# Attention phase of a Flamingo block: order of statistics, normalisation, residual and x transposes within a step

## What is computed

```python
x = x + tanh(g_xattn) * attention(layernorm(x), ctx, ctx, w_q, w_k, w_v, w_o)
x = x + tanh(g_ffn)   * ffn(layernorm(x), w_gate, w_up, w_down)

def attention(query, key, value, ...):
    scores  = q @ k.T * SCALE + causal mask (k_pos <= q_pos)
    weights = softmax(scores)
    return (weights @ v) @ w_o

def ffn(x, ...):                       # act_qdq: to 16-bit steps of the tensor's maximum and back
    up   = act_qdq(act_qdq(x) @ dequant4(w_up).T)
    gate = act_qdq(act_qdq(x) @ dequant4(w_gate).T)
    o    = act_qdq(act_qdq(gate * sigmoid(gate)) * up)
    return o @ dequant4(w_down).T
```

## Time and profile before

| | |
|---|---|
| three runs | 1492.4, 1486.42, 1490.44 us; median 1490.44 |
| the profiled execution | 1487.6 us, its span 1485.8 us |
| busy over the span: TensorE, VectorE, ScalarE, GpSimd | 89%, 69%, 43%, 17% |
| mean granted TensorE clock | 0.956 of full |
| TensorE's waits for another engine, 0 to 560 us, the three largest | 13.3, 9.2 and 6.9 us |

### The profile page before, as it was taken

The page is one execution under the profiler, slowest core; times in us unless marked ns, Lnnn a source line. Parts: engine busy times, 40 slices in busy tenths (PEclk is TensorE's granted clock), DMA queues, the critical chain, the costliest instruction groups (busy, mean ns, idle before and its releaser), DMA issues. The chain is left out here.

```text
span 1485.8 us, 18879 instructions
## 1 busy us (share of the span) xinstructions
PE 1328.3 (89%) x6142; PEld 1086.8 (73%) x6142; DVE 1021.9 (69%) x1397; ACT 644.8 (43%) x769; POOL 255.1 (17%) x312
## 2 busy tenths in 40 slices
PE   7899999999999978999999999999992029999999
PEld 6677767768777866888888778878882018888887
DVE  0467667856866655777777679998998984545453
ACT  2434334334333324333333255556667973333331
POOL 1124214313312220001000034550110000000000
PEclk9999999999999998999999999999996559999999
DMA  8013202312322435666764889986558863454543
GB/s 311 1 36 100 93 30 92 99 42 71 106 70 69 171 123 209 246 238 237 247 240 159 271 295 311 319 311 214 174 202 334 316 223 116 161 167 150 176 145 118
DMA packets 111248, 259.77 MB, mean 175 GB/s; under 512 B 10832, under 2 KB 23120, under 8 KB 109648
## 3 DMA queue, kind: packets, MB, share of 16 engines
q1 hardware_dynamic: 110896, 259.04, 50.3%
q10 hardware_dynamic: 288, 0.00, 0.0%
HBM read 152.04 MB, written 106.95 MB: 174 GB/s over the span
## 5 line engine op out<-in xcount | busy, mean ns | idle before, releaser
L1096 PE MATMUL gpG<-xph,Wh 128*128 128x512 f32 x384 | 153.0, 398 | 6.0 <-DVE xpl L1020 6.0
L1570 PE MATMUL pD<-Wh,xph 128*128 128x512 f32 x384 | 150.7, 392 | 4.6 <-DVE xpl L1549 4.6
L1096 PE MATMUL pU<-xph,Wh 128*128 128x512 f32 x384 | 150.8, 393 | 1.7 <-POOLq L63 1.0
L1096 PE MATMUL gpG<-xph,Wl 128*128 128x512 f32 x384 | 150.8, 393 | 0.0
L1096 PE MATMUL gpG<-xpl,Wh 128*128 128x512 f32 x384 | 150.6, 392 | 0.0
L1570 PE MATMUL pD<-Wh,xpl 128*128 128x512 f32 x384 | 150.5, 392 | 0.0
L1570 PE MATMUL pD<-Wl,xph 128*128 128x512 f32 x384 | 150.5, 392 | 0.0
L1096 PE MATMUL pU<-xpl,Wh 128*128 128x512 f32 x384 | 150.2, 391 | 0.0
L1096 PE MATMUL pU<-xph,Wl 128*128 128x512 f32 x384 | 150.1, 391 | 0.0
L1549 DVE TENSOR_TENSOR xpl<-doq,xph 128x1536 fp32r<-128x1536 int16 (+1 forms) x34 | 56.4, 1663 | 123.1 <-ACT xph L1516 123.1
L1003 ACT ACTIVATE gst<-gpG,sc 128x512 f32<-128x512 f32 x96 | 66.3, 691 | 168.3 <-PE gpG L1096 168.3
(11 more groups left out here) (172 smaller groups left out, 2930.5 us busy)
## 6 DMA issues: line engine op xcount, KB each, us to landing
dub<-up_d SPq DMA_DIRECT2D x42, 768.0 KB, 4.7
gate_d<-gst SPq DMA_DIRECT2D x96, 256.0 KB, 2.3
gb<-gate_d SPq DMA_DIRECT2D x32, 768.0 KB, 6.3
up_d<-ust SPq DMA_DIRECT2D x96, 256.0 KB, 4.3
xr<-xn_d SPq DMA_DIRECT2D x9, 1024.0 KB, 6.0
xph<-up_d SPq DMA_DIRECT2D x11, 768.0 KB, 6.2
xpl<-up_d SPq DMA_DIRECT2D x11, 768.0 KB, 6.0
xin<-in_x SPq DMA_DIRECT2D x32, 256.0 KB, 2.7
```

Of the source, the lines that this page charges most:

```text
L1096: mm = pe.matmul(ps[:, :], Ws[:, it, kt * P:(kt + 1) * P], xs[:, kt, :], start=(kt == 0 and Ws is Wh and xs is xh), stop=(kt == KT - 1 and ...
L1570: mm = pe.matmul(pD[4 * t + q][:, :], os_[n][:, cs], Ws[:, it, :], start=(it == 0 and os_ is oh and Ws is Wh), stop=(it == IT - 1 and os_ ...
```

## The change

Six orders within a step are changed. GpSimd does `rstd` of tile k+2 ahead of that of tile k-3. ScalarE normalises tile k+2 directly after the probability copies and the job's copy, no longer at the end of the step. VectorE takes the statistics of tile k+2 at the head of the step, and in an A-chunk step the residual ahead of them; the sums come ahead of the job's scale; in a chunk step all corrections come ahead of `largest`. TensorE turns x ahead of the values in an A-chunk step too, with one wait more, ahead of the second chunk, for the second half of `pTl`.

```diff
--- before.py
+++ after.py
@@ -507,10 +507,10 @@
                 pool.tensor_scalar(rs_[:, n, 2:3], mv_[:, n, 0:1], rs_[:, n, 1:2], -1.0, ALU.mult, ALU.mult).then_inc(rstd_s, 1)
 
             def step(b, k, have, jobs):
+                if have(k + 2):
+                    rstd(b, k + 2, mv, rs, mean_done, eps_done, rstd_done, xn_done)
                 if have(k - 3):
                     rstd(b, k - 3, mv2, rs2, mean2_done, eps2_done, rstd2_done, x2_done)
-                if have(k + 2):
-                    rstd(b, k + 2, mv, rs, mean_done, eps_done, rstd_done, xn_done)
                 if have(k - 1):
 
                     j = k - 1
@@ -547,6 +547,11 @@
                 q = job_at(k, jobs, 2)
                 if q is not None:
                     job_hi(act, J, b, q)
+                if have(k + 2) and k + 2 >= 2:
+                    j = k + 2
+                    act.wait_ge(*tile(rstd_done, b, j))
+                    act.wait_ge(*tile(xT_ps, b, j - 2))
+                    normal(b, j, xn, xin[j % BQ], mv, rs, xn_done)
 
                 def exponentials():
                     if have(k - 1):
@@ -561,18 +566,13 @@
                         act.wait_ge(*tile(s_ps, b, j - 2))
                         act.activation(xh[j % 2][:, :], pX[:, :], ACT.Copy).then_inc(xh_done, 1)
 
-                def normals():
+                def normal2():
                     if have(k - 3):
                         j = k - 3
                         act.wait_ge(*tile(rstd2_done, b, j))
                         act.wait_ge(*at(x2_out[j % 2], 8 * BQ * b, 16 * (j // 2)))
                         act.wait_ge(*tile(x2max_done, b, j - 2))
                         normal(b, j, x2, x1[j % 2], mv2, rs2, x2_done)
-                    if have(k + 2) and k + 2 >= 2:
-                        j = k + 2
-                        act.wait_ge(*tile(rstd_done, b, j))
-                        act.wait_ge(*tile(xT_ps, b, j - 2))
-                        normal(b, j, xn, xin[j % BQ], mv, rs, xn_done)
 
                 if which != 0:
                     exponentials()
@@ -588,7 +588,7 @@
                         act.activation(Vh[:, n, :], pT[:, (n % 2) * 512:(n % 2 + 1) * 512], ACT.Copy).then_inc(ch_hi, 1)
                 if which == 0:
                     high()
-                normals()
+                normal2()
 
             def copied(dst, src, ready, count, done):
                 act.wait_ge(ready, count)
@@ -689,6 +689,10 @@
                     for _ in range(min(n, len(chunks))):
                         chunks.pop(0)()
 
+                if which == 0 and have(k - 3):
+                    residual(b, k - 3)
+                if have(k + 2) and k + 2 >= 2:
+                    statistics(b, k + 2)
                 if have(k - 2):
                     j = k - 2
                     for h, cs in enumerate(halves):
@@ -699,7 +703,7 @@
                     job_lo(dve, J, b, q)
 
                 early = which is not None or not have(BQ)
-                if early and have(k - 3):
+                if early and which != 0 and have(k - 3):
                     residual(b, k - 3)
                 if have(k - 1):
                     scores_down(b, k - 1)
@@ -708,16 +712,13 @@
                 q = job_at(k, jobs, 1)
                 if q is not None:
                     job_integer(dve, J, b, q)
-                if which == 0:
-                    some(2)
-                if have(k + 2) and k + 2 >= 2:
-                    statistics(b, k + 2)
-                some(2 if which == 0 else 1)
+                if which is not None:
+                    some(4 if which == 0 else 1)
+                if have(k - 1):
+                    sums(b, k - 1)
                 q = job_at(k, jobs, 0)
                 if q is not None:
                     job_scale(dve, J, b, q)
-                if have(k - 1):
-                    sums(b, k - 1)
                 some(2 if which == 0 else 3)
                 if which == 0:
                     some(8)
@@ -726,10 +727,9 @@
                     dve.wait_ge(*tile(xh_done, b, j))
                     dve.wait_ge(*tile(s_ps, b, j - 2))
                     dve.tensor_tensor(xl[j % 2][:, :], pX[:, :], xh[j % 2][:, :].bitcast(F32), ALU.subtract).then_inc(xl_done, 1)
-                some(2)
+                some(8)
                 if have(k - 3):
                     largest(b, k - 3)
-                some(8)
 
             for j in range(2):
                 statistics(0, j)
@@ -783,6 +783,9 @@
                         if p == PAIRS - 1:
                             mm.then_inc(o_ps, 1)
                     if which is not None:
+                        if p == 1 and have(j):
+
+                            pe.wait_ge(*part(pTl_done, b, j, 1))
                         chunk(b, ahead, which, p)
 
             def scores(b, k):
@@ -827,13 +830,11 @@
                             mm = pe.transpose(pX[:, kt * P:(kt + 1) * P], xn[j % 2][:, kt * P:(kt + 1) * P], ident[:, :])
                         mm.then_inc(xT_ps, 1)
 
-                if which != 0:
-                    if have(k) and k >= 0:
-                        scores(b, k)
-                    turn_x()
+                if which != 0 and have(k) and k >= 0:
+                    scores(b, k)
+                turn_x()
                 values(b, k, have)
                 if which == 0:
-                    turn_x()
                     scores(b, k)
                 q = job_at(k, jobs, 1)
                 if q is not None:
```

## The result

The changed kernel takes 1483.24 us (median of 20 runs, 1477.66 to 1489.47), the kernel before 1489.87 (20 runs, 1485.38 to 1492.99). The ratio is 0.996, interval 0.9947 to 0.9972: 0.4% faster, 6 us.

What follows compares the result with a forecast made beforehand. TensorE's own queue was taken to set the attention phase, so its waits matter. The terms, -6.3 - 5.5 + 1.4 + 3.4 - 0.6 = -7.6 us, against the median 1490.4 gave 1482.8 us; range 1478.5 to 1487.5.

Steps and rivals of the forecast that it cites:

- 0.5% line: About 0.5% (7.5 us) is what a measurement can tell from no change; the forecast lay right on it.
- Plain steps, 6.3: Attention phase: eleven of TensorE's twelve waits for GpSimd's product of the probabilities go, 6.3 us gained.
- two moves shorten: Plain steps: statistics to the step's head and scale behind the sums start GpSimd's product about 2 us earlier.
- V-chunk step, 5.5: End of V-chunk step: corrections go ahead of the maximum, TensorE waits less; 1.8 us gained, three times, 5.5 us.
- it just fits: After the V-chunk step: residual ready at 206.1 to 206.9, TensorE wants it at 207.2, some 0.3 us to spare.
- Cover of 1.5 us: Plain steps: VectorE's idle time before the first probability correction hides the moved statistics, with 1.5 us of cover left.
- third rival: VectorE becomes the bound: correction late in 18 plain steps; 1 us beyond the cover gives +10 us, 1500.8; chance 0.07.
- A-chunk step, 1.4: A-chunk steps: x transposes wait for the weight job's low part, stall 3.4 us; 0.45 us lost, three times, 1.4 us.
- Prologue, 3.4: Step 0: ScalarE's A copies wait behind tile 2's normalisation, TensorE's third chunk is late; 3.4 us lost, bounds 0 and 5.
- Clock, -0.6: Attention phase: fewer lower-clock stretches after V stalls, more after A and prologue stalls; -0.6 us, bounds -5.1 and +3.4.
- first rival: The clock takes it back: all three A stalls and the prologue's fall to the lower level; 1485.1 us, chance 0.17.
- second rival: More is won: A stalls leave the clock alone, none falls in the prologue; -12 us at most, 1480, chance 0.2.

## Why the prediction came out right, and where its terms did not

The time was forecast at 1482.8 and measured at 1483.24; as a difference -7.6 against -6.6 of the medians, or -6 by the ratio, whose interval reaches from -4 to -8. The 0.5% line was where I had put it, and it fell on the side of "within". But the sum is better than its terms. The two gains came out 3.4 us smaller together than forecast, because two costs were left out, the scale's slow row and the jump at the loop's head. On the other side the prologue may have cost up to 1.7 us less. By the terms as measured below the sum at full clock would be -5.5 to -3.9, against the -7.0 that I had without the clock. That the total came as near as it did is partly luck.

- **Plain steps, 6.3.** A round's four intervals between residuals add up to 53.79 us before (12.31, 13.81, 13.86, 13.81) and 51.98 after (12.26, 13.33, 13.20, 13.19): 1.8 us a round, 5.4 in all. The mechanism was right. The step that failed is "two moves shorten": one of them, the swap, cost. I priced the moved scale by its old duration, and beside GpSimd's product it is another.
- **V-chunk step, 5.5.** The stall went from 2.82 to 0.90 us as worked out. The sentence "it just fits" for the residual of step 10 held. What failed is that I followed the lateness one step and not to the loop's head, one step further, where TensorE now waits 2.0 and 2.1 us in two of three rounds. By intervals at full clock, from the residual of step 9 over the head to that of step 4, it was 50.8 us and is 50.3 in these two rounds, a gain of 0.5 each; in the last round, with no jump behind it, step 9 to the last batch's first step went from 35.45 to 33.46, a gain of 2.0 where 1.8 was forecast. So the term was 3.0 in all. With VectorE's rounds written out the two waits are gone.
- **Cover of 1.5 us.** Right for steps within a round. Wrong at its head, where the 5.19 us of VectorE's idle time before the correction looked like waiting for ScalarE: it stood about as long as at the jumps above, and started 0.75 us later than the copy allowed, so there was no cover at all. This is the third rival, VectorE as the bound, in 2 of the 18 steps, and it is the sign of being wrong that I had named, a wait for the residual in plain steps.
- **A-chunk step, 1.4.** The stall was forecast at 3.4 and is 3.48 us, with the forecast releaser; the stall of 2.2 us with x turned late shows that 1.3 us of it is the x transposes' wait for the low part. By intervals at full clock (7.05 + 25.82 with rounds written out, 10.32 + 22.16 with the step undone) the edits of this step cost 0.4 a step, 1.2 in all.
- **Prologue, 3.4.** First scores at 14.85 us behind the x transposes in the kernel with VectorE's rounds written out, 11.50 undone: 3.35, one stretch of 3.4 us at the lower clock included, so between 1.7 and 3.35 without it. In the profiled run of the change it was 5.1, with 6.4 us at the lower clock.
- **Clock, -0.6.** The mean clock over the runs is the same as before's, so about 0. The first rival is what the profiled run shows: the prologue's stall and the A stalls went with a fall. Its six stretches, against four or five forecast, cost up to 7 us more than before's; that is beyond my bound of +3.4, for which I had counted no stretch longer than 3.4 us. (The bound itself does not follow from my counts either: all A stalls and the prologue's make +1.7, as in the first rival.) Other runs of the same program escape, at clock 0.958, and take 1478 us, the second rival. I had treated the fall as a property of a stall; over runs it is a chance, and the spread of the times (12 us, before 8) is its price.
- **Behind the attention phase**, where the programs are the same, I had called a different span a sign of being wrong. From the first gate product to the end it is 922.2 us before and 923.8 after, and 919.8 to 925.8 in the other kernels; so this says nothing, and the profiled times of two kernels differ by some us for such reasons alone.

The Trainium skill has a sentence on each of the two effects I missed. Advanced Engine Details and Errata, VectorE Performance Modes, says that VectorE's second port to SBUF is shared with GpSimd, so that VectorE's instructions in a two-port mode and GpSimd's block each other. The trace agrees: the scale's second row, both sides in SBUF (that it runs in such a mode no run shows), starts at 103.31 inside GpSimd's product and ends with it (104.75 and 104.72), twelve times, and takes 0.17 where none runs; the reduction ahead of it does not stretch. Runtime: NRT & Kernel Launch, Instruction fetch mechanics, says that a taken branch to a place outside the fetched window has to wait for its instructions. The trace agrees in place (5.3 us at both jumps back, none with the rounds written out); the section gives no time for it, and that it is the fetch no run here shows.

## What to carry to other kernels

In a kernel whose engines run a loop of their own, look at the first instructions after the jump back apart from the rest: idle time there that is put down to another engine may be the jump's own, and nothing should be put ahead of what others wait for. Move one instruction at a time for one wait: here the residual's move alone gained 1.45 us in each A-chunk step, and with the statistics, the x transposes and the normalisation moved as well the step took 0.4 us longer than in the old order. Before a small VectorE instruction is moved beside a long GpSimd one, look for a place in the trace where the two already run together.

## What the hardware showed that I had not expected

- VectorE stood 5.27 and 5.40 us at the jump back to the head of its loop, and 5.43 us in another kernel; written out, it had no such wait, and the kernels were 4 to 7 us shorter at full clock.
- A VectorE row on 128 x 16 elements took 1.44 us instead of 0.17 while GpSimd's 1.90 us product ran, twelve times of twelve.
- One program's runs lie between 1477.66 us at a mean clock of 0.958 and 1489.47 us at 0.952.
